# Softmax stage of a macaron transformer block: 64-row tiles for the scores, two-bank slots for the maximum stream, and PV issued for two steps together

## What is computed

```python
qkv = x @ W_qkv.T + b_qkv
q, k, v = jnp.split(qkv, 3, axis=-1)          # 16 heads of 16 each
scores = jnp.einsum('bqhe,bkhe->bhqk', q, k) * scale
causal = jnp.tril(jnp.ones((l, l), dtype=bool))
scores = jnp.where(causal[None, None], scores, -jnp.inf)
attn = jax.nn.softmax(scores, axis=-1)
out = jnp.einsum('bhqk,bkhe->bqhe', attn, v)
...
x = x + 0.5 * ffn(layernorm(x))
x = x + attention(layernorm(x))
x = x + 0.5 * ffn(layernorm(x))
```

## Time and profile before

| | us |
|---|---|
| three runs: median (lowest, highest) | 1540.11 (1534.96, 1540.85) |
| the profiled execution's own time | 1542.46 |
| its span on the core | 1540.8 |
| mean granted clock of TensorE | 0.901 |
| PE, PEld busy | 1325.7 (86%), 1003.7 (65%) |
| DVE, ACT, POOL busy | 1019.6 (66%), 775.6 (50%), 496.9 (32%) |
| softmax stage, first memset to last output copy's end | 503.3 to 1099.3 |

### The profile page before, as it was taken

One profiled execution on the slowest core, in us unless ns is written; L12 is line 12 of the kernel. 1 busy time (PEld: TensorE's weight loads), 2 busy tenths in 40 slices (PEclk: granted clock), 3 DMA queues, 4 the chain that ended last, 5 costly groups with the idle time before them and its releaser, 6 DMA issues. The chain is left out here.

```text
span 1540.8 us, 31184 instructions
## 1 busy us (share of the span) xinstructions
PE 1325.7 (86%) x8678; PEld 1003.7 (65%) x8709; DVE 1019.6 (66%) x2335; ACT 775.6 (50%) x1949; POOL 496.9 (32%) x651
## 2 busy tenths in 40 slices
PE   2628999899699499999998999999778269998998
PEld 1417999799588255555555555554465159997998
DVE  6594555499866777767675777773286755554787
ACT  2524556333244046666675666666546236564333
POOL 1554444255300201222211112212324554443454
PEclk9658999899899569999998999999896569999999
DMA  6503434122465712223322222200315114433233
GB/s 188 169 3 97 123 123 122 60 73 74 146 233 231 136 30 43 44 43 66 61 44 44 43 43 43 44 2 1 114 35 167 55 59 124 123 123 93 83 112 106
DMA packets 86509, 135.73 MB, mean 88 GB/s; under 512 B 12992, under 2 KB 66176, under 8 KB 83328
## 3 DMA queue, kind: packets, MB, share of 16 engines
q1 hardware_dynamic: 64896, 90.29, 22.1%
q0 software_dynamic: 13056, 35.67, 8.3%
q10 hardware_dynamic: 8448, 8.39, 1.6%
HBM read 81.35 MB, written 52.43 MB: 87 GB/s over the span
## 5 line engine op out<-in xcount | busy, mean ns | idle before, releaser
L1448 DVE TENSOR_REDUCE s_MX<-s_ps_a 128x1 f32<-128x512 f32 (+4 forms) x624 | 368.9, 643 | 133.8 <-PE s_ps_a L1515 132.2
L1422 ACT ACTIVATE s_PR<-s_ps_b 128x512 f32<-128x512 f32 (+3 forms) x768 | 343.7, 491 | 162.3 <-PE s_ps_b L1537 155.2
L1515 PE MATMUL s_ps_a<-s_KO,s_QO 96*128 96x512 f32 (+3 forms) x768 | 286.1, 422 | 22.7 <-DMA s_QO<-qk_scratch 22.7
L1537 PE MATMUL s_ps_b<-s_QO,s_KO 98*128 98x512 f32 (+3 forms) x768 | 266.6, 368 | 7.2 <-issue 3.9
L1391 POOL TENSOR_SCALAR_AFFINE_SELECT s_PR<-s_PR 128x256 f32<-128x256 f32 x256 | 103.5, 407 | 474.5 <-ACT s_PR L1422 473.6
L1537 PEld LDWEIGHTS s_ps_b<-s_QO,s_KO 98*128 98x128 f32 x768 | 146.3, 194 | 72.6 <-ACT s_PR L1422 54.4
L603 POOL DMA_INDIRECT f_XG<-xn_scratch,f_tok_u x144 | 136.4, 947 | 167.3 <-PE f_ps_x L700 157.4
L1515 PEld LDWEIGHTS s_ps_a<-s_KO,s_QO 96*128 96x128 f32 x768 | 152.1, 211 | 28.7 <-DVE s_MX L1448 20.8
L810 POOL DMA_INDIRECT f_YG<-y_scratch,f_slots_u x128 | 121.0, 945 | 150.2 <-DVE X L885 94.6
L1552 PE MATMUL s_ps_o<-s_PR,s_VG 128*17 128x512 f32 (+3 forms) x1536 | 163.0, 496 | 5.3 <-POOL s_PR L1391 5.3
L656 DVE TENSOR_TENSOR f_xl<-f_ps_x,f_xh 128x256 fp32r<-128x256 f32 x144 | 61.1, 425 | 97.7 <-ACT f_xh L628 92.6
(11 more groups left out here) (206 smaller groups left out, 2966.9 us busy)
## 6 DMA issues: line engine op xcount, KB each, us to landing
y_scratch<-f_YS SPq DMA_DIRECT2D x144, 128.0 KB
s_KO<-qk_scratch SPq DMA_DIRECT2D x48, 256.0 KB, 5.8
s_QO<-qk_scratch SPq DMA_DIRECT2D x96, 128.0 KB, 6.6
xn_scratch<-f_XN ACTq DMA_DIRECT2D x16, 512.0 KB, 3.2
qk_scratch<-p_QKh SPq DMA_DIRECT2D x32, 256.0 KB
qk_scratch<-p_QKl SPq DMA_DIRECT2D x32, 256.0 KB
f_stage<-in_w_up SPq DMA_DIRECT2D x20, 352.0 KB
X<-in_x SPq DMA_DIRECT2D x4, 1024.0 KB, 9.4
```

Of the source, the lines that this page charges most:

```text
L1422: nc.scalar.activation(PR[:, u // 2 % SLOTS, u % 2, 0:W - lo], ps_b[u % RING][:, lo:W], ACT.Exp, scale=SCALE).then_inc(exp_done, 1)
L1448: nc.vector.tensor_reduce(MX[:, h:h + heads, i, s], ps_a[v % RING][:, 0:heads * keys].rearrange("p (h n) -> p h n", h=heads), AX.X, ALU.ma ...
L1515: last = nc.tensor.matmul(ps_a[v % RING][:, at:at + keys], QO[k][0:R, h, i * P:(i + 1) * P], KO[k][0:R, h % 2, s * W:s * W + keys], start= ...
L1537: nc.tensor.matmul(ps_b[u % RING][:, lo:W], KO[k][0:RM, h % 2, i * P:(i + 1) * P], QO[k][0:RM, h, hf * W + lo:(hf + 1) * W], start=True, s ...
```

## The change

The scores are computed on two row tiles of 64 partitions (`TILE`). Each head has its own 48 rows (50 with the maximum's), even heads from partition 0 and odd ones from 64; `QO` shrinks to two tiles and needs no zeros. `KO`'s rows of ones are set together with others by memsets of 32 partitions. An A unit covers one or two head pairs (`hp`) and writes a slot of two banks, one for each row tile; DVE reads both banks in one instruction, so a group has 21 units. `ps_a` is two such slots. There is no `ps_t`: the three transposes of a group (`turn_max`, twice `turn_output`) take their turn in the same two slots, by a table `USES` of 24 uses a group, and one semaphore `slot_read` counts the reads of all of them. The mask above the diagonal takes four small matmuls, two for each row tile. PV is issued for two steps together, after steps 2, 4, 6, 8, 10 and 11. The transposes stand behind the second head of their step rather than the fourth. The loads are 12 DMAs a group rather than 9, the placement of the maximum 4 rather than 2.

```diff
+            wide = min(W // keys, 2)
+            A_UNITS += [(i, s, hp, wide, keys) for hp in range(0, 2, wide)]
...
+    for n in range(NB):
+        beside = [("a",) + one for one in A_BESIDE[n]]
+        USES += beside[:1]
+        if n == 1:
+            USES.append(("out", -1, 1))
+        if n == OUT_T:
+            USES.append(("out", 0, 0))
+        if n == MAX_T:
+            USES.append(("max", 1, 0))
+        USES += beside[1:]
...
-        ps_a = [ps(f"ps_a{i}", [P, W]) for i in range(RING)]
+        ps_a = [ps(f"ps_a{i}", [P, 2, W]) for i in range(2)]
         ps_b = [ps(f"ps_b{i}", [P, W]) for i in range(RING)]
         ps_o = ps("ps_o", [P, W])
-        ps_t = ps("ps_t", [P, W])
...
+            for k in range(4):
+
+                for c in range(2):
+                    rows = slice(c * TILE + 32, (c + 1) * TILE)
+                    nc.vector.memset(KO[k][rows, :, :].bitcast(F32), 1.0).then_inc(ones, 1)
...
+                    for c in range(2):
+                        dve.wait_ge(a_done[c], NA * g + v + 1)
+                    _, slot = slot_of_a(g, v)
+                    scores = ps_a[slot][:, :, 0:heads * keys].rearrange("p c (h n) -> p c h n", h=heads)
+                    nc.vector.tensor_reduce(MX[:, :, hp:hp + heads, i, s], scores, AX.X,
+                                            ALU.max).then_inc(slot_read, 1)
...
-                    if v >= RING or since(g, 1):
-                        pe.wait_ge(a_read, NA * g + v + 1 - RING)
+                    if not isinstance(g, int) or q >= 2:
+                        pe.wait_ge(slot_read, q - 1)
...
+                        for j in range(2):
+                            for c in range(2):
+                                rows = slice(c * TILE, (c + 1) * TILE)
+                                scores = banks[c][:, 0:heads * keys].rearrange("p (h n) -> p h n", h=heads)
+                                nc.tensor.matmul(scores[:, :, keys - P + j * TILE:keys], identb[rows, j, :],
+                                                 neg[rows, 0:heads, 0:P - j * TILE],
+                                                 start=j == 0, stop=False, skip_group_check=True)
+                    for hp in range(hp0, hp0 + heads):
+                        at = (hp - hp0) * keys
+                        for c in range(2):
+                            rows = slice(c * TILE, c * TILE + R)
+                            last = nc.tensor.matmul(banks[c][:, at:at + keys], QO[k][rows, hp, i * P:(i + 1) * P],
+                                                    KO[k][rows, hp, s * W:s * W + keys], start=not diagonal,
+                                                    stop=True, skip_group_check=True)
...
-                        if h == GH - 1:
-                            if n >= 1:
-                                pv_step(g, k, n - 1)
+                        if h == 1:
                             if n == 1 and since(g, 1):
                                 turn_output(g - 1, 1)
-                            if n == MAX_T - 1:
+                            if n == OUT_T:
                                 turn_output(g, 0)
                             if n == MAX_T and until(g, 1, NG):
                                 turn_max(g + 1)
+                        if h == GH - 1 and n >= 2 and n % 2 == 0:
+                            pv_step(g, k, n - 2)
+                            pv_step(g, k, n - 1)
...
+                pv_step(g, k, NB - 2)
                 pv_step(g, k, NB - 1)
```

More of the change, by code:

```diff
@@ L1258, in softmax_stage, with slot_use, slot_of_a @@
     MAX_T = 1 + max(n for n in range(NB) if (1, NA - 1) in A_BESIDE[n])
+    OUT_T = MAX_T - 1
+    USES = []
+    for n in range(NB):
[8 more added lines that the diff above has]
+        USES += beside[1:]
+    NU = len(USES)
+    FIRST = NA + 1 + AHEAD
+    def slot_use(g, what, ahead, index=0):
+        at = USES.index((what, ahead, index))
+        if not isinstance(g, int):
+            return FIRST - 1 + NU * g + at, (FIRST - 1 + at) % 2
+        q = FIRST + sum(0 <= n + use[1] < NG for n in range(g + 1) for use in USES[:at if n == g else NU])
+        return q, q % 2
+    def slot_of_a(g, v):
+        if isinstance(g, int) and g * NA + v < NA + AHEAD:
+            q = v + g * (NA + 1)
+            return q, q % 2
+        ahead = 1 if v >= AHEAD else 2
+        return slot_use(g - ahead, "a", ahead, v)
     SLOTS = 6
-    LOAD = 9 * 16
-    PLACE = 2 * 16
-    assert GH == 4 and D // G == 64 and GH * NB % RING == 0 and NB * 2 % SLOTS == 0 and MAX_T < NB
+    LOAD = 12 * 16
+    PLACE = 4 * 16
+    assert GH == 4 and D // G == 64 and GH * NB % RING == 0 and NB * 2 % SLOTS == 0 and MAX_T < NB and NU % 2 == 0
+    assert all(len(A_BESIDE[n]) <= GH for n in (1, OUT_T, MAX_T))
     with ExitStack() as c:
@@ L1315, in softmax_stage, with max_slot, out_slot @@
         recip = sem("recip")
-        att_done = sem("att_done")
         block = c.enter_context(nc.Block())
+        def max_slot(g):
+            return (NA, NA % 2) if isinstance(g, int) and g == 0 else slot_use(g - 1, "max", 1)
+        def out_slot(g, hf):
+            return slot_use(g + hf, "out", -hf, hf)
         def turn(g, k, back):
@@ L1474, in normalise, with a_beside @@
                     turned[:, :, :, 0:HD], RC[:, :, :].unsqueeze(3).to_broadcast([P, 4, GH, HD]),
-                    ALU.mult).then_inc(att_done, 1)
+                    ALU.mult).then_inc(slot_read, 1)
+            def a_beside(g, groups, v):
+                if until(g, groups, NG):
+                    a_units(g + groups, [v])
+                    if v == NA - 1:
+                        combine(g + 1)
             a_units(0, range(NA))
@@ L1493, in _ @@
                         max_low(g + 1)
+                    for groups, v in A_BESIDE[n][1:]:
+                        a_beside(g, groups, v)
             normalise(NG - 1, 3, 1)
@@ L1507, in a_units @@
                     if diagonal:
-                        scores = ps_a[v % RING][:, 0:heads * keys].rearrange("p (h n) -> p h n", h=heads)
-                        nc.tensor.matmul(scores[:, :, keys - P:keys], identb[:, :], neg[:, 0:heads, :],
-                                         start=True, stop=False, skip_group_check=True)
-                    for h in range(h0, h0 + heads):
-                        at = (h - h0) * keys
-                        last = nc.tensor.matmul(ps_a[v % RING][:, at:at + keys], QO[k][0:R, h, i * P:(i + 1) * P],
-                                                KO[k][0:R, h % 2, s * W:s * W + keys], start=not diagonal,
-                                                stop=True, skip_group_check=True)
```

153 lines of the change are left out of this document (71 added, 82 removed).

## The result

| | before | after |
|---|---|---|
| median of 4 runs (lowest, highest), us | 1540.48 (1534.96, 1543.17) | 1656.95 (1643.5, 1660.0) |
| ratio after to before, 95% interval | | 1.0744 (1.0678 to 1.081) |
| span of the profiled execution, us | 1540.8 | 1655.5 |
| mean granted clock | 0.901 | 0.808 |
| first memset of the stage | 503.3 | 499.0 |

What follows compares the result with a forecast made beforehand. TensorE was taken as the limit, closely coupled to VectorE and ScalarE. A group of 35.1 us against 33.73 gave +20 us over 15 groups, less 5 for start and last group: +15, forecast 1556 us, range 1502 to 1600.

Steps and rivals of the forecast that it cites:

- the main case: Softmax stage: waits for the two slots outweigh TensorE's savings, +15 us, 1556 us; chance 0.33 for 1548 to 1575.
- rival 3: TensorE in the steady part falls to 1.2 GHz for a quarter of the time: +45 us, 1600 us; chance 0.20.
- Row tiles: A pass: a pair of matmuls runs side by side in 0.24 us, taking 5.8 us a group from TensorE.
- rival 4: A pass: row tiles run one after the other, a pair costing 0.48 us: 1593 us; chance 0.08.
- The chain without slot waits: One group's exponentials, B matmuls and paired PV, with no wait for a slot: 27.5 us.
- The slot waits: A units and transposes sharing two slots delay B matmuls and exponentials: 7.6 us a group, 3.6 from S7 to S9.
- PV in pairs: PV in six visits for twelve saves about 0.3 us each, 1.8 us of TensorE a group.
- Reads: VectorE's maxima: 21 reads for 39 save 1.2 us; 2 x 512 lasts 1.22 us and repeats after 1.13.
- The period at the full clock: Steady group: chain of 27.5 us plus slot waits of 7.6 makes 35.1 us against 33.73.
- rival 5: VectorE alone bounds the kernel, reading without pause, 22.9 us a group: 1375 us; chance 0.02.
- The start: Stage start: shorter memsets bring the first load 1.7 us earlier and VectorE sets the A phase; -5 us with the last group.
- the 12 DMAs "at nothing": Loads at the start: 12 DMAs for 9 move the same bytes, hidden in the 12 us they take to land.

Runs made afterwards that it cites:

- experiment 7: Changed kernel with the loads of groups 2 and 3 issued after the placement of group 0's maximum: 1633.93 us.
- experiment 4: PV issued for each step alone: in the changed kernel 1616.4, 1624.33 and twice 1642.4 us; in that kernel with scores on 128 rows 1595.74 us.
- experiment 1: Changed kernel with the scores on all 128 rows again, keeping its slots, order and paired PV: 1585.07 us, ratio 1.0351.
- Experiment 2: Changed kernel with each B matmul over 114 rows in place of 50, summing two heads' scores: 1610.83 us, ratio 1.0516.
- experiment 6: Each maximum read over only the first 64 columns of a key range: 1536.36 us with scores on 128 rows, 1494.89 us in the changed kernel.
- experiment 5: Kernel before the change with only PV issued for two steps together: 1517.35 us, ratio 0.9904.
- 3, B twice: Changed kernel with the B matmuls of the second and third head issued twice: 1611.54 us.

## Why the prediction was wrong

- **Sign right, size wrong.** Slower was forecast, +15 us for +116. The step that failed is the choice between the main case and rival 3, and the size of rival 3. I summed every price at the full clock and gave the fall of the clock 0.20, "a quarter of the time" and 3 us a group. It is half the time: 20.5 of 41.0 us. Groups with 10.2 us cold take 37.6 (experiment 7), those with 20.5 take 41.0: 0.33 us for each cold us (0.31 in experiment 4), so about 34.2 with none, and the clock costs 6.8 us a group. The price was about right (3 us for a quarter of 35 us is 0.34 for each); the share of the time was not. By an estimate from these numbers the clock costs some 95 us over 14 groups, and without it the kernel would stand near 1560. The 34.2 is a line drawn on, not a measured group; the 34.0 of experiment 4, with single PVs, stands beside it.
- **Rival 3's sign was in the profile.** It stood in the earlier trace rows: 1.2 GHz through an A phase with TensorE busy nine tenths. I used it to name the rival, then took "a quarter of the time" from no row.
- **Row tiles: right.** The two matmuls of a pair start 3 to 4 ns apart, and a pair costs what one matmul costs in its place: behind a wait it is 0.34 us to the next B (756.62 to 756.96 in the change), as behind PV in the earlier trace rows. So rival 4's 0.48 falls. But the 5.8 us saved were worked out wrongly: of the 24 pairs of a group half have fewer than 512 columns, 384 is their mean, and 9216 columns at 0.24 for 512 are 4.3 us; 3.4 came through (experiment 4). The Trainium skill's "TensorE: Matmul & The Clock Gate", Part 3, reports 3.07 times for four row tiles. By that a pair would cost an estimated 0.31 us. In the change no pair of 512 columns at the full clock has its next matmul sooner than 0.33 us, so the bare 0.24 isn't seen and no run decides between the two. What I left out is that B matmuls lie on one tile each, so B, mask and A matmuls that follow each other start together too. PE's timeline:

```profile
736.48 0.54 PE L1593 MATMUL s_ps_b<-s_QO,s_KO 50*128 50x512 f32 x1
736.49 0.29 PE L1563 MATMUL s_ps_a<-s_neg,s_identb 64*128 64x128 bf16 x2
```

- **The chain without slot waits: right.** 27.5 us forecast; the last group takes 27.36 in experiments 1 and 2, and the whole group 29.5 with short reads (which still take their turns), at the full clock in all three.
- **The slot waits: right in kind, too large.** I had 7.6 us; 34.2 - 29.5 is 4.7, and 3.6 with full rows. The period at the full clock, 35.1, was 1 us high. What the sum lacked is the clock, which is back at 1.00 with short reads (experiment 6); whether it is the stops themselves that bring it down isn't shown.
- **PV in pairs: right in kind, too large.** I had 1.8 us of TensorE a group. It is 1.1 in the kernel before and 0.2 with two slots and full rows; in the change the pairs cost 29 us in all, with less time at the full clock (experiment 4).
- **Reads: right.** Four in a row, 4.35 us for one of 768 columns and three of 1024, fit 1.22 for the length and 1.13 for the pitch. VectorE alone is no bound: it is busy for 23.2 us of a group of 41 and waits 237 us in all, so rival 5 falls. The Trainium skill's "TensorEngine Tiling (Array Packing)", PSUM Bottleneck, says that tiling does not speed up the evacuation of PSUM. Here the evacuation is no bound on throughput; it matters through two slots instead of three banks.
- **The start: wrong, and the part that came true was luck.** The first A matmul was forecast near 519.5 and came at 518.5. But the whole stage began 4.4 us earlier in this run (498.96 against 503.33), as it did in a run whose stage starts with the unchanged code (498.33 in experiment 5), and the first load was 15.5 us ahead of that matmul instead of 12. B was to start near 550 and started at 558.2. Counted from the first memset that is 59.2 us against 51.4 before: 5 less was forecast, 7.9 more was measured. I had costed the 12 DMAs "at nothing" and the placement as "hidden"; both were one wait of 8.2 us behind the loads.

What stays open: why the clock falls, and which of filled rows, overlap of neighbours, stops and the density of the work weighs how much in it. Experiment 2 shows that filled rows and lost overlap together bring it back, experiment 6 that short reads do. In experiment 4 the same kernel has groups at either level.

## What to carry to other kernels

Where TensorE is busy all the time at the full clock, saving some of its work can cost the clock: look for a stretch of the same trace that is at 1.2 GHz while TensorE is busy, and price every matmul of the new version at both levels before summing. Keep what gives TensorE less to switch (PV in pairs) apart from what makes it wait (fewer PSUM slots); the first was worth 1.0% alone. Ask of each load that is cut into more DMAs how large its packets become, and what short transfer queues behind it.

## What the runs showed that I had not expected

- More work for TensorE, or the same columns on more rows, made the kernel faster three times, each against the kernel before on its chip: 64 us (experiment 1), 39 us (2) and 38 us (3, B twice, a single run).
- The edit that shortens the reads took 3.6 us off a group that was at the full clock anyway, and 11 or more off the change's, where it also brought the clock back.
- One kernel, with PV for each step alone, had a group of 34.0 us at 1.00 and then one of 45.0 at 0.61.
- Matmuls for unlike purposes (B, mask, A) on different row tiles started 10 ns apart at 736.48, and a matmul over both tiles behind a pair on single tiles started 0.41 us after it, where a B on one tile starts 0.34 after it.
